# Turning fp16 halves with DMA transposes on the SP queue instead of fp32 rows on TensorE

## The chip, the cores and the metric

The kernel runs on one core of one Trainium2 chip. Its time is the device time of one launch in microseconds (us); the kernel before takes 1377.87 us, the median of 3 runs (1377.47 to 1381.09). Engines are named as in the profile: PE is TensorE's matmul, PEld its weight load, DVE is VectorE, ACT is ScalarE, POOL is GpSimd, SP is SyncE, which here only waits and issues DMAs.

## The reference

16 sequences of 256 tokens with 512 channels, 4096 tokens in all. First a recurrence over the tokens of each sequence (WKV) with the normalised rows as keys and a context as values, added to x. Then, on the normalised result, a shared gated MLP and a routed mixture of 8 experts, of which each token takes 2, with at most 1280 tokens per expert.

```python
x = x + tanh(g_xattn[0]) * wkv(time_decay, time_first, k=layernorm(x), v=ctx_2048)
n = layernorm(x)                                   # (4096, 512)
logits = n @ router                                # (4096, 8)
topk_logits, sel = top_k(logits, 2); cw = softmax(topk_logits)
# row -> (expert, slot), slots in token order, kept while slot < 1280
h = silu(gate) * up;  gate, up = split(buf[e] @ w_up_gate[e])      # 512 -> 2 x 352
routed = sum over the token's 2 experts of cw * (h @ w_down[e])    # 352 -> 512
shared = (silu(gate_s) * up_s) @ shared_w_down                     # 512 -> 2 x 1408 -> 512
x = x + tanh(g_ffn[0]) * (routed + shared)
```

## The kernel before

Tokens are worked in 32 tiles of 128 rows, 8 groups of 4 tiles. Each large product is made from fp16 halves: a value is split into a high fp16 part and the rest (`lo`), and three matmuls (hi·hi, hi·lo, lo·hi) stand for one fp32 product. So the normalised rows are wanted channel-major (channels on the partitions) and split: `xT[:, par, hi/lo, kt, token]`, with two buffers `par` for two groups.

**The attention stage** (up to about 770 us) is a software pipeline that is written out by hand. `group(gs, ga, ...)` on each engine runs the shared MLP of group `gs` and at the same time the recurrence, second norm and routing of group `ga = gs + 1`. It has 15 steps: 11 `up_pair` steps of 24 matmuls of 512 columns and 4 `down_tile` steps of 33. `tiles_at(stage, step)` says which tile does which stage in a step; a tile comes every 3 steps. On PE `attend(done)` puts the small work of the pipeline between the matmuls: at `done == 0` `turn_x` (stage 6), `logits` (stage 7) and `turn_v` (stage 2), at `MID` (18) `turn_y` (stage 4), at `LATE` (21) `turn_k` (stage 0). Each `turn` is 4 fp32 transposes on PE into one of two PSUM banks: `PT` for keys, y and x, `PR` for v and the logits.
After the second norm (`normalise_x2`, DVE, into `xln`) a tile goes: `turn_x` on PE into `PT`, `x_hi` on ACT (`PT` to the high half of `xT`), `x_lo` on DVE (`PT` minus high half), then `logits`, then `choose_experts` on DVE, which reads the logits out of `PR`. The next user of `PR`, `turn_v`, waits for that read (`logits_taken`). SP stores `xln` to DRAM as fp32 rows (`xln_d`) for the experts, and loads x and the context ahead.

**The expert stage** (about 820 to 1320 us) works 8 experts of 1280 slots, each as 5 chunks (`EC`) of 256 slots, 40 chunks in all. POOL gathers 128 rows of a slot tile from DRAM by index (`gather_rows`, line 468), six slot tiles ahead, into two buffers `xg`: even tiles in `wkv`, odd ones in `srng`. A gather waits until the tile two before it in the same buffer has been turned (`xg_turned`). PE runs `up_chunk(j+1)`, `turn_slots(j+2)`, `down_chunk(j)`. `gather_hi` (ACT) and `gather_lo` (DVE) empty the turned rows from `PT`/`PR` into `xgT`. ACT scales each output tile into `ostage` (`stage_out`, line 653), and POOL adds it to `moe_d` in DRAM by an indirect DMA (line 487), in program order with the gathers: gather of tile s+6, wait for staged tile s, add tile s, wait until the add of tile s-1 has landed.
The weights of the next expert come in 11 pieces (`q` = 0 to 10; 8 of `w_up_gate`, 3 of `w_down`) through two staging buffers `wst`: SP loads piece q when piece q-2 has been split (`load_chunk`), ACT makes its high half (`weights_hi`), DVE its low half (`weights_lo`). ACT's and DVE's program in chunk j is: piece 3j, hidden part 0 of chunk j+1, piece 3j+1, hidden part 1, piece 3j+2, hidden part 2, and then `stage_out` of chunk j. SP has nothing else to do in this stage.

At the end the second half of the last group's MLP runs (`half_ups(1)`), and the sum is copied out.

Of the kernel before, what the change touches and what calls it, by code (L numbers as in the profile page):

```python
# [50 lines left out]
MID, LATE = 18, 21  # L51
# [3 lines left out]
def build(nc, x, ctx_in, g_x, g_f, t_decay, t_first, router, w_ug, w_dn, s_ug, s_dn, out):  # L55
    es = ExitStack()
    with es:
# [9 lines left out]
        xln_d = nc.dram_tensor("xln_d", (NTOK, D), F32, kind="Internal").ap()  # L67
# [34 lines left out]
        decay = carve(KT * SEG).rearrange("p (k s) -> p k s", k=KT)  # L102

# [9 lines left out]
        xg1 = carve(D)  # L113
# [3 lines left out]
        xg = [xg1, srng[:, 1, :]]  # L117
        xgT = xT[:, 0, :, :, :].rearrange("p h k (r t) -> p r h k t", r=2)
        sums = wkv[:, 0:HT * D].rearrange("p (j c) -> p j c", j=HT)

# [10 lines left out]
        rt_f = sb("rt_f", [P, KT, E], F32)  # L131
# [24 lines left out]
        sprod = sb("sprod", [P, 2, GT, E], F32)  # L156
        posk = sb("posk", [P, 2, GT], F32)
# [13 lines left out]
        dve_waits = sem("dve_waits"); pool_waits = sem("pool_waits")  # L171
# [12 lines left out]
        x_turned = sem("x_turned"); xhi_ready = sem("xhi_ready"); xlo_ready = sem("xlo_ready")  # L184
# [12 lines left out]
        xg_turned = sem("xg_turned"); xg_hi = sem("xg_hi"); xg_lo = sem("xg_lo")  # L197
# [48 lines left out]
        def _(sp):  # L246
            def load_x(c, k):

                sp.dma_start(acc_tile(c), x_rows[bass.ds(c * P, P), :]).then_inc(x_in[k], 16)
# [4 lines left out]
            def attn_group(g, sums, last=False):  # L254


                for k in range(GT):
# [6 lines left out]
                    sp.wait_ge(xln_ready, c + 1)  # L264
                    sp.dma_start(xln_d[bass.ds(c * P, P), :], xln[k % 2]).then_inc(xln_stored[k % 2], 16)
# [19 lines left out]
            attn_group(0, False)  # L285
# [3 lines left out]
            attn_group(1, False)  # L289
            with sp.Fori(2, GROUPS - 1) as n:  # L290
                attn_group(n, True)
            attn_group(GROUPS - 1, True, last=True)
# [17 lines left out]

            for q in range(WCH):
                load_chunk(0, 0, q)
                if q == 1:
                    start_sums(GROUPS - 2)
            for q in range(WCH):
                load_chunk(1, 1, q)
            with sp.Fori(1, E // 2) as i:
                for p in range(2):
                    for q in range(WCH):
                        load_chunk(2 * i + p, p, q)  # L320
# [24 lines left out]
        def _(pool):  # L345
# [110 lines left out]
            for r in range(2):  # L456
                pool.wait_ge(xln_stored[r], 16 * TILES // 2)
            pool.sem_inc(stage_free, 2)
# [6 lines left out]
            def gather_rows(e, p, s, first):  # L465
                if not first:
                    wait_alone(xg_turned, ET * e + s - 1)
                pool.indirect_dma_start(  # L468
                    out=xg[s % 2], out_offset=None, in_=xln_d,
# [38 lines left out]
        def _(act):  # L508
# [57 lines left out]
            def group(gs, ga, gpar, first=False, last=False):  # L566

                for s in steps_of(first):
                    if ga is not None:
                        for k in tiles_at(6, s):  # L570
                            x_hi(ga, k, first, 1 - gpar)
# [53 lines left out]
            def gather_hi(e, p, j):  # L625

                cc = EC * e + j
                for t in range(2):
                    act.wait_ge(xg_turned, 2 * cc + t + 1)
                    if not (isinstance(e, int) and cc < 2):  # L630
                        act.wait_ge(eup_ready, IT * (cc - 1))
                    T = (PT, PR)[t]
                    act.activation(xgT[:, (p + j) % 2, 0, :, t * P:(t + 1) * P],
                                   T[:, :].rearrange("p (k t) -> p k t", k=KT), ACT.Copy).then_inc(xg_hi, 1)

# [19 lines left out]
            def expert(e, p, half, last=False):  # L655


                for j in range(EC):
# [8 lines left out]
                    if j + 2 < EC:  # L667
                        gather_hi(e, p, j + 2)
                    elif not last:
                        gather_hi(e + 1, 1 - p, j + 2 - EC)  # L670
# [3 lines left out]
            gather_hi(0, 0, 0)  # L674
# [5 lines left out]
            gather_hi(0, 0, 1)  # L680
# [11 lines left out]
        def _(pe):  # L692
# [8 lines left out]
            def turn_k(c, k, first):  # L701
# [3 lines left out]
                elif not (first and k == 0):  # L705
                    pe.wait_ge(xlo_ready, c if k == GT else c - 1)
# [13 lines left out]
            def turn_y(c, k):  # L720
# [3 lines left out]
                else:  # L724
                    pe.wait_ge(xlo_ready, c)
                turn(PT, nd[:, 0].rearrange("p k t -> p (k t)")).then_inc(y_turned, 1)

            def turn_x(c, k):
                pe.wait_ge(xln_ready, c + 1)
                turn(PT, xln[k % 2]).then_inc(x_turned, 1)  # L730

            def logits(g, k, par, route):

                c = GT * g + k
                pe.wait_ge(xlo_ready, c + 1)
# [75 lines left out]
            def group(gs, ga, gpar, first=False, split=False, last=False):  # L811
                if gs is not None:
                    pe.wait_ge(xlo_ready, GT * gs + GT)
                for s in steps_of(first):
# [3 lines left out]
                    if gs is None:  # L818
                        for done in (0, MID, LATE):
# [20 lines left out]
            def turn_slots(e, p, j):  # L840
                cc = EC * e + j
                for t in range(2):
                    s = 2 * j + t
                    pe.wait_ge(gathered[t], 16 * cc + 16)
                    if not isinstance(e, int) or cc > 0:
                        pe.wait_ge(xg_lo, 2 * cc)
# [469 lines left out]
```

## Time and profile before

| | |
|---|---|
| median of the runs | 1377.87 us (1377.47 to 1381.09) |
| span of the profiled execution, first to last instruction | 1378.7 us |
| PE busy | 1276.0 us, 93% |
| DVE busy | 824.8 us, 60% |
| ACT busy | 457.5 us, 33% |
| POOL busy | 477.8 us, 35% |
| TensorE clock granted | 0.996 of full, mean |

The times of the runs surround the span of the profiled execution: its 1378.7 us lie 0.8 us above the median, and nothing that needs adding lies around it. Busy time is a union of intervals for each engine. A timeline row is: start, length, engine, line, operation, tiles out and in, count, and in brackets the idle time before it with the work that ended it. A row of the chain of waits is start, length, what. On DMA rows the last number is the median from issue to landing.

### The profile page before, as it was taken

How to read it: one execution, taken by the hardware profiler on the slowest of the kernel's cores; microseconds unless marked ns; L12 is line 12 of the kernel's file. 1: busy time of each engine (PE TensorE's matmuls, PEld its weight loads, DVE VectorE, ACT ScalarE, POOL GpSimd, SP SyncE). 2: the span in 40 equal slices, each digit the busy share in tenths (PEclk: the TensorE clock that was granted, in tenths of full speed). 3: DMA queues.
4: the chain of work that ended last, by engine and by line, in shares of the span. 5: the costliest groups of instructions: out<-in, count | busy, mean ns of one | idle time of the engine just before them, and what ended most of it. 6: DMA issues, size and time to landing. Idle time of an engine off the chain costs nothing. (4 is left out here: it accounts for less than half of the span.)

```text
span 1378.7 us, 22718 instructions
## 1 busy us (share of the span) xinstructions
PE 1276.0 (93%) x8139; PEld 805.4 (58%) x8139; DVE 824.8 (60%) x1615; ACT 457.5 (33%) x840; POOL 477.8 (35%) x461
## 2 busy tenths in 40 slices
PE   1267999999999999999999899999999999999999
PEld 1233444444444444444444667778778777877766
DVE  6988868768678688688687434343434344343312
ACT  3324214223123133133141224444444444444321
POOL 5533142242232232421421313344434443443320
PEclk9999999999999999999999999999999999999999
DMA  7322012021021111120010324465556555554455
GB/s 203 120 84 77 31 25 68 31 70 46 10 70 46 24 55 45 24 77 32 9 54 26 66 78 107 102 139 112 122 109 132 110 118 120 117 121 93 85 122 183
DMA packets 67195, 112.62 MB, mean 82 GB/s; under 512 B 9166, under 2 KB 30694, under 8 KB 66961
## 3 DMA queue, kind: packets, MB, share of 16 engines
q0 software_dynamic: 20064, 42.19, 16.8%
q1 hardware_dynamic: 37376, 62.67, 15.0%
q10 hardware_dynamic: 9648, 6.31, 1.7%
q8 instruction: 71, 1.16, 0.4%
q14 instruction: 36, 0.29, 0.1%
HBM read 72.19 MB, written 46.81 MB: 86 GB/s over the span
## 5 line engine op out<-in xcount | busy, mean ns | idle before, releaser
L771 PE MATMUL PU<-xT,wreg 128*128 128x512 f16 x1848 | 420.6, 381 | 0.1
L771 PEld LDWEIGHTS PU<-xT,wreg 128*128 128x128 f16 x1848 | 179.4, 98 | 194.5 <-issue 3.2
L786 PE MATMUL PD<-wreg,hreg 128*128 128x512 f16 x924 | 204.8, 379 | 0.0
L487 POOL DMA_INDIRECT moe_d<-hreg,eidx x80 | 126.6, 1582 | 111.9 <-ACT hreg L653 92.5
L866 PE MATMUL PU<-xT,wkv 128*128 128x256 f16 (+1 forms) x1440 | 160.5, 273 | 3.5 <-DVE xT L1215 2.4
L866 PE MATMUL PU<-xT,hreg 128*128 128x256 f16 (+1 forms) x1440 | 160.5, 273 | 0.0
L866 PEld LDWEIGHTS PU<-xT,wkv 128*128 128x128 f16 (+1 forms) x1440 | 146.2, 106 | 19.6 <-issue 3.5
L866 PEld LDWEIGHTS PU<-xT,hreg 128*128 128x128 f16 (+1 forms) x1440 | 146.5, 106 | 15.6
L786 PEld LDWEIGHTS PD<-wreg,hreg 128*128 128x128 f16 x924 | 89.1, 98 | 103.0
L1224 DVE SCALAR_TENSOR_TENSOR srng<-PU,srng 128x256 f32<-128x256 f32 (+1 forms) x120 | 50.8, 423 | 164.1 <-ACT srng L644 164.0
L695 PE MATMUL PT<-ident,wkv 128*128 128x128 f32 x384 | 65.3, 297 | 80.7 <-DVE wkv L1036 33.7
L564 ACT ACTIVATE hreg<-srng 128x512 f16<-128x512 f32 x77 | 48.5, 630 | 210.9 <-DVE srng L1081 210.9
L384 POOL TENSOR_TENSOR rstd<-ve,mhalf 128x1 f32<-128x1 f32 x64 | 38.0, 593 | 230.5 <-DVE ve L990 230.4
L695 PEld LDWEIGHTS PT<-ident,wkv 128*128 128x128 f32 x384 | 48.7, 151 | 107.7 <-DVE wkv L1036 41.4
L468 POOL DMA_INDIRECT wkv<-xln_d,eidx x40 | 39.4, 985 | 203.6 <-PE PR L849 190.9
L1033 DVE RECIPROCAL wkv<-wkv 128x512 f32<-128x512 f32 x32 | 107.2, 3350 | 0.2
L644 ACT ACTIVATE srng<-PU 128x256 f32<-128x256 f32 (+1 forms) x120 | 45.8, 382 | 155.3 <-PE PU L866 155.3
L1026 DVE TENSOR_TENSOR_SCAN wkv<-wkv 128x516 f32<-128x516 f32 x64 | 96.6, 1509 | 1.1
L1227 DVE TENSOR_TENSOR wkv<-srng,wkv 128x256 f16<-128x256 f32 (+1 forms) x120 | 50.9, 424 | 57.9 <-ACT wkv L646 57.9
L880 PE MATMUL PD<-hreg,wkv 128*128 128x512 f16 (+1 forms) x360 | 81.1, 379 | 0.9 <-ACT hreg L653 0.9
L653 ACT ACTIVATE hreg<-PD,wslot 128x512 f32<-128x512 f32 x80 | 55.0, 687 | 79.2 <-PE PD L880 72.2
L880 PE MATMUL PD<-wkv 128*128 128x512 f16 (+1 forms) x360 | 81.1, 379 | 0.0
(141 smaller groups left out, 1547.7 us busy)
## 6 DMA issues: line engine op xcount, KB each, us to landing
wkv<-in_L_ffn_w_up_gate SPq DMA_DIRECT2D x64, 176.0 KB, 3.5
acc<-in_x SPq DMA_DIRECT2D x32, 256.0 KB, 3.9
wkv<-in_ctx SPq DMA_DIRECT2D x32, 256.0 KB, 3.7
xln_d<-wkv SPq DMA_DIRECT2D x32, 256.0 KB, 2.0
moe_d<-acc SPq DMA_DIRECT2D x7, 1024.0 KB, 5.1
wkv<-in_L_ffn_w_down SPq DMA_DIRECT2D x16, 256.0 KB, 4.8
acc<-n_L_ffn_shared_w_up_gate ACTq DMA_DIRECT2D x14, 256.0 KB, 3.3
out<-moe_d SPq DMA_DIRECT2D x1, 3584.0 KB, 26.3
```

The lines of the kernel that those rows point to most:

```text
L487: pool.indirect_dma_start(out=moe_d, out_offset=bass.IndirectOffsetOnAxis(ap=eidx[:, p, 1, s:s + 1], axis=0), in_=ostage[s % 2], in_offset ...
L564: act.activation(hh[:, m, 0, :], srng[:, r, :], ACT.Copy).then_inc(hhi_ready, 1)
L653: act.activation(ostage[t], PD[t][:, :], ACT.Copy, scale=wslot[:, bass.ds(2 * cc + t, 1)]).then_inc(ostaged, 1)
L695: mm = pe.transpose(dst[:, kt * P:(kt + 1) * P], src[:, kt * P:(kt + 1) * P], ident[:, :])
L771: mm = pe.matmul(PU[r][gu][:, :], sU[:, m, gu, a, kt, :], xT[:, gpar, b, kt, :], start=(kt == 0 and a + b == 0), stop=(kt == KT - 1 and a ...
L786: mm = pe.matmul(PD[t % 2][:, :], hh[:, j, a, t * P:(t + 1) * P], sD[:, j, b, :], start=(j == 0 and a + b == 0), stop=(j == JT - 1 and a = ...
L866: mm = pe.matmul(PU[r][gu][0:M, 0:CH], eU[p][:, gu, a, kt, m * P:m * P + M], xgT[:, (p + j) % 2, b, kt, :], start=(kt == 0 and a + b == 0) ...
L880: mm = pe.matmul(PD[t][:, :], eh[0:M, (p + j) % 2, m, a, t * P:(t + 1) * P], eD[p][0:M, m, b, :], start=(m == 0 and a + b == 0), stop=(m = ...
L1026: dve.tensor_tensor_scan(scan_out[:, n].rearrange("p k s -> p (k s)"), decay.rearrange("p k s -> p (k s)"), scan_in[:, n].rearrange("p k s ...
L1033: dve.reciprocal(nd[:, 1], nd[:, 1]).then_inc(rcp_done, 1)
L1224: dve.scalar_tensor_tensor(out=esr[r][0:M, :], in0=PU[r][1][0:M, 0:CH], scalar=HS / WS, in1=esr[r][0:M, :], op0=ALU.mult, op1=ALU.mult).th ...
L1227: dve.tensor_tensor(eh[0:M, (p + j) % 2, m, 1, :], esr[r][0:M, :], eh[0:M, (p + j) % 2, m, 0, :], ALU.subtract).then_inc(ehlo_ready, 1)
```

## The change

The normalised rows are split first and turned afterwards, by DMA.

In the attention stage ACT copies `xln` to fp16 (`x_hi`) and DVE subtracts (`x_lo`), both row-major, into `xhl`, 1024 fp16 values a row. SP then issues a DMA transpose from `xhl` straight into `xT` (8 blocks of 128 by 128 in one instruction) and stores `xhl` to DRAM (`xhl_d`, as many bytes a row as before). `turn_x` is gone from PE. `logits` waits for the transpose to have landed and stands at `EARLY` (9 matmuls into its step) instead of 0; `choose_experts` on DVE stands at the end of its step's attention work instead of at the start; `turn_k` and `turn_y` wait for `x2_done` instead of `xlo_ready` on `PT`.

In the expert stage the gathers bring rows of `xhl_d`, and SP turns each gathered tile with a DMA transpose (`turn_rows`). `turn_slots`, `gather_hi` and `gather_lo` are gone from PE, ACT and DVE. SP's weight loads are now written between its transposes, in its program order.

```diff
-        xln_d = nc.dram_tensor("xln_d", (NTOK, D), F32, kind="Internal").ap()
+        xhl_d = nc.dram_tensor("xhl_d", (NTOK, 2 * D), F16, kind="Internal").ap()
...
-                    sp.wait_ge(xln_ready, c + 1)
-                    sp.dma_start(xln_d[bass.ds(c * P, P), :], xln[k % 2]).then_inc(xln_stored[k % 2], 16)
+                    wait_alone(xlo_ready, c + 1)
+                    if k == 0 and has_past:
+                        wait_alone(up_ready, JT * (g - 1))
+                    sp.dma_start_transpose(
+                        xT[:, par, :, :, k * P:(k + 1) * P].rearrange("p h k t -> p (h k) t"),
+                        xhl[k % 2]).then_inc(x_turned[k % 2], 16)
+                    sp.dma_start(xhl_d[bass.ds(c * P, P), :], xhl[k % 2]).then_inc(xln_stored[k % 2], 16)
...
+            def turn_rows(e, p, j, first=False):
+
+                cc = EC * e + j
+                if not first:
+                    wait_alone(eup_ready, IT * (cc - 1))
+                for t in range(2):
+                    wait_alone(gathered[t], 16 * cc + 16)
+                    sp.dma_start_transpose(
+                        xgT[:, (p + j) % 2, :, :, t * P:(t + 1) * P].rearrange("p h k t -> p (h k) t"),
+                        xg[t]).then_inc(xg_turned[t], 16)
...
+            def expert_pair(e):
+                for p in range(2):
+                    for j in range(EC):
+                        if j + 2 < EC:
+                            turn_rows(e + p, p, j + 2)
+                        else:
+                            turn_rows(e + p + 1, 1 - p, j + 2 - EC)
+                        for q in range(IT * j + 2, min(IT * j + 2 + IT, WCH)):
+                            load_chunk(e + p + 1, 1 - p, q)
+                    for q in range(2):
+                        load_chunk(e + p + 2, p, q)
...
             def gather_rows(e, p, s, first):
                 if not first:
-                    wait_alone(xg_turned, ET * e + s - 1)
+                    wait_alone(xg_turned[s % 2], 16 * (EC * e + s // 2))
...
-            def x_hi(g, k, first, par):
+            def x_hi(g, k, first):
...
-                act.wait_ge(x_turned, c + 1)
-                act.activation(xT[:, par, 0, :, k * P:(k + 1) * P], PT[:, :].rearrange("p (k t) -> p k t", k=KT),
-                               ACT.Copy).then_inc(xhi_ready, 1)
+                act.wait_ge(xln_ready, c + 1)
...
+                act.activation(xhl[k % 2][:, 0:D], xln[k % 2], ACT.Copy).then_inc(xhi_ready, 1)
...
-                    pe.wait_ge(xlo_ready, c if k == GT else c - 1)
+                    pe.wait_ge(x2_done, c if k == GT else c - 1)
...
-                if done == 0:
-                    for k in tiles_at(6, s):
-                        turn_x(GT * ga + k, k)
+                if done == EARLY:
                     for k in tiles_at(7, s):
                         logits(ga, k, par, not first)
+                if done == 0:
                     for k in tiles_at(2, s, last):
                         turn_v(ga, k, first)
...
-            def turn_slots(e, p, j):
...
-                pe.wait_ge(xg_lo, 2 * cc + 2)
+                for t in range(2):
+                    pe.wait_ge(xg_turned[t], 16 * (cc + 1))
...
-                    for k in tiles_at(7, s):
-                        choose_experts(GT * ga + k)
                     for k in tiles_at(6, s):
-                        x_lo(GT * ga + k, k, par)
+                        x_lo(GT * ga + k, k)
...
                         weigh_and_scan(GT * ga + k, k, first)
...
+                    for k in tiles_at(7, s):
+                        choose_experts(GT * ga + k)
```

What DVE does in step 4 of a group in the kernel before; L1063 is the first operation of the choice, which frees `PR`, L1041 the adding of the attention result, L1000 the normalising of keys:

```order
L1081 SCALAR_TENSOR_TENSOR srng<-PU,srng 128x512
L1063 TENSOR_REDUCE lt<-PR 128x8
L1065 MAX top<-lt 128x8
...
L1088 TENSOR_TENSOR hreg<-srng,hreg 128x512
...
L1041 SCALAR_TENSOR_TENSOR acc<-PT,gates,acc 128x512
L986 BN_STATS bn<-acc 128x6
...
L1000 TENSOR_SCALAR wkv<-acc,mv,rstd 128x512
```

The same step of DVE in the changed kernel; L1095, L1102, L1058, L1003, L1017 and L1077 are the former L1081, L1088, L1041, L986, L1000 and L1063:

```order
L1095 SCALAR_TENSOR_TENSOR srng<-PU,srng 128x512
L1102 TENSOR_TENSOR hreg<-srng,hreg 128x512
...
L1058 SCALAR_TENSOR_TENSOR acc<-PT,gates,acc 128x512
L1003 BN_STATS bn<-acc 128x6
...
L1017 TENSOR_SCALAR wkv<-acc,mv,rstd 128x512
L1077 TENSOR_REDUCE lt<-PR 128x8
L1079 MAX top<-lt 128x8
```

The choice, which led the step, now stands behind the adding of the attention result and everything that follows from it.

What SP does in the expert stage of the kernel before, at the head of its loop over pairs of experts (L305 loads a piece of `w_up_gate`):

```order
L305 DMA wkv<-in_L_ffn_w_up_gate 128x352
L305 ISA
L305 DMA wkv<-in_L_ffn_w_up_gate 128x352
L301 REGISTER_ALU
L305 ISA
L305 DMA wkv<-in_L_ffn_w_up_gate 128x352
```

And at the same place in the changed kernel (L334 is the transpose of a gathered tile, L321 the load of a piece):

```order
L334 DMA_TRANSPOSE xT<-wkv 128x8x128
L334 DMA_TRANSPOSE xT<-srng 128x8x128
L317 ISA
L321 ISA
L321 DMA wkv<-in_L_ffn_w_up_gate 128x352
L317 REGISTER_ALU
L321 ISA
L321 DMA wkv<-in_L_ffn_w_up_gate 128x352
```

Pieces 2, 3 and 4 (then 5 to 7, then 8 to 10) now stand behind two transposes, the second of which waits for a gathered odd tile (`srng`).

## Rows read from the trace of the kernel before

**Rows 1.** The page: busy time of each engine, share of the span, instructions.

```profile
PE 1276.0 (93%) x8139; PEld 805.4 (58%) x8139; DVE 824.8 (60%) x1615; ACT 457.5 (33%) x840; POOL 477.8 (35%) x461
```

**Rows 2.** Busy time by stretch: one group of the attention stage, the expert stage.

```profile
168.30:264.90 96.60, 93.96 (x496) 46.77 (x495) 75.17 (x146) 25.84 (x37) 29.95 (x32) 1.00 0.16 45
840.00:1320.00 480.00, 479.75 (x3720) 376.84 (x3719) 186.37 (x378) 211.76 (x454) 198.93 (x164) 1.00 0.55 113
```

**Rows 3.** PE's waits in 160 to 740 us: us in total, times, longest.

```profile
PE PT L695 <- DVE xT L1057: 8.5, 7, 1.4
PE PT L695 <- DVE wkv L1036: 6.3, 10, 1.0
```

**Rows 4.** Timeline of PE, steps 3 to 5 of a group.

```profile
401.70 0.60 PE L695 MATMUL PT<-ident,wkv 128*128 128x128 f32 x4
402.13 4.70 PE L771 MATMUL PU<-xT,wreg 128*128 128x512 f16 x21
...
413.32 0.66 PE L695 MATMUL PT<-ident,wkv 128*128 128x128 f32 x4 [0.32 <-DVE wkv L1036]
...
415.10 0.60 PE L695 MATMUL PR<-ident,wkv 128*128 128x128 f32 x4
```

**Rows 5.** Timeline of DVE in the same steps.

```profile
406.80 0.69 DVE L1057 TENSOR_TENSOR xT<-PT,xT 128x512 f16<-128x512 f32 x1 [1.18 <-ACT xT L553]
...
413.78 0.16 DVE L1063 TENSOR_REDUCE lt<-PR 128x8 f32<-128x16 f32 x1
...
415.56 0.75 DVE L1041 SCALAR_TENSOR_TENSOR acc<-PT,gates,acc 128x512 f32 x1
...
417.69 0.55 DVE L1000 TENSOR_SCALAR wkv<-acc,mv,rstd 128x512 f32 x1
```

**Rows 6.** Chain of waits in one chunk of the expert stage: start, length, what.

```profile
957.47 7.86 PE PU L866 x72
965.33 0.44 PE PT L849 x4
965.77 0.44 PE PR L849 x4
966.21 3.89 PE PD L880 x18
```

**Rows 7.** Timeline of ACT and POOL in a chunk.

```profile
1052.83 0.63 ACT L623 ACTIVATE wkv<-wkv 128x512 f16<-128x512 f32 x1 [0.41 <-DMA wkv<-in_L_ffn_w_down]
...
1053.76 0.38 ACT L644 ACTIVATE srng<-PU 96x256 f32<-96x256 f32 x1 [0.29 <-PE PU L866]
...
1054.62 0.42 ACT L646 ACTIVATE wkv<-srng 96x256 f16<-96x256 f32 x1 [0.49 <-DVE srng L1224]
...
1056.67 0.69 ACT L653 ACTIVATE hreg<-PD,wslot 128x512 f32<-128x512 f32 x1 [0.67 <-PE PD L880]
...
1058.20 1.59 POOL L487 DMA_INDIRECT moe_d<-hreg,eidx  x1 [2.23 <-ACT hreg L653]
...
1060.10 1.30 POOL L468 DMA_INDIRECT srng<-xln_d,eidx  x1 [0.30 <-issue]
```

**Rows 8.** DMA issues of the expert stage: count, KB each, us to landing.

```profile
wkv<-in_L_ffn_w_up_gate SPq DMA_DIRECT2D x51, 176.0 KB, 3.6
wkv<-in_L_ffn_w_down SPq DMA_DIRECT2D x14, 256.0 KB, 5.0
...
wkv<-xln_d,eidx POOLq DMA_INDIRECT x37, 3.4
srng<-xln_d,eidx POOLq DMA_INDIRECT x36, 4.5
```

**Rows 9.** DMA issues of the whole run, 256 KB each.

```profile
acc<-in_x SPq DMA_DIRECT2D x32, 256.0 KB, 3.9
...
xln_d<-wkv SPq DMA_DIRECT2D x32, 256.0 KB, 2.0
```

**Rows 10.** Timeline of PE: the first two chunks of products.

```profile
831.04 8.03 PE L866 MATMUL PU<-xT,wkv 128*128 128x256 f16 x72 [2.38 <-DVE xT L1215]
```

More of the change, by code:

```diff
@@ L183, in build @@
         xln_stored = [sem(f"xln_stored{r}") for r in range(2)]
-        x_turned = sem("x_turned"); xhi_ready = sem("xhi_ready"); xlo_ready = sem("xlo_ready")
+        x_turned = [sem(f"x_turned{r}") for r in range(2)]; xhi_ready = sem("xhi_ready"); xlo_ready = sem("xlo_ready")
         logits_ready = sem("logits_ready"); logits_taken = sem("logits_taken"); top_steps = sem("top_steps")
@@ L196, in build @@
         gathered = [sem(f"gathered{r}") for r in range(2)]
-        xg_turned = sem("xg_turned"); xg_hi = sem("xg_hi"); xg_lo = sem("xg_lo")
+        xg_turned = [sem(f"xg_turned{r}") for r in range(2)]
         ew_in = [sem(f"ew_in{r}") for r in range(2)]
@@ L288, in _ @@
                          zeros[:, :].unsqueeze(1).to_broadcast([P, (HT + 2) * KT, P])).then_inc(moe_started, 16)
[L289 to L292, printed above, removed]
+            attn_group(1, False, 1, has_past=False)
+            with sp.Fori(1, GROUPS // 2 - 1) as n:
+                attn_group(2 * n, True, 0)
+                attn_group(2 * n + 1, True, 1)
+            attn_group(GROUPS - 2, True, 0)
+            attn_group(GROUPS - 1, True, 1, last=True)
             def load_chunk(e, p, q):
@@ L314, in _ @@
                     start_sums(GROUPS - 2)
-            for q in range(WCH):
+            sp.wait_ge(up_ready, JT * GROUPS)
+            for j in range(2):
+                turn_rows(0, 0, j, first=True)
+            for q in range(2):
                 load_chunk(1, 1, q)
[L317 to L320, printed above, removed]
+            with sp.Fori(0, E // 2 - 1) as i:
+                expert_pair(2 * i)
+            expert(E - 2, 0)
+            expert(E - 1, 1, last=True)
             for r in range(2):
@@ L812, in group @@
                 if gs is not None:
-                    pe.wait_ge(xlo_ready, GT * gs + GT)
+                    for r in range(2):
+                        pe.wait_ge(x_turned[r], 16 * (GT // 2 * gs + GT // 2))
                 for s in steps_of(first):
@@ L837, in _ @@
             group(GROUPS - 2, GROUPS - 1, 0, last=True)
-            def turn_slots(e, p, j):
[L841 to L846, printed above, removed]
-                    T = (PT, PR)[t]
-                    for kt in range(KT):
-                        mm = pe.transpose(T[:, kt * P:(kt + 1) * P], xg[s % 2][:, kt * P:(kt + 1) * P], ident[:, :])
-                    mm.then_inc(xg_turned, 1)
             def up_chunk(e, p, j):
@@ L890, in expert @@
                         up_chunk(e + 1, 1 - p, 0)
-                    if j + 2 < EC:
-                        turn_slots(e, p, j + 2)
-                    elif not last:
-                        turn_slots(e + 1, 1 - p, j + 2 - EC)
                     down_chunk(e, p, j)
@@ L1239, in expert @@
                             expert_hidden(e + 1, 1 - p, 0, m)
-                    if j + 2 < EC:
-                        gather_lo(e, p, j + 2)
-                    elif not last:
-                        gather_lo(e + 1, 1 - p, j + 2 - EC)
             def half_hidden(h, m):
```

86 lines of the change are left out of this document (36 added, 50 removed).

## The prediction, made before the changed kernel ran

> **What bounds the kernel now.** I read the page first: PE is busy 93% of the span, no other engine over 60% [rows 1]. Split by stretch, a group of the attention stage has a period of 96.6 us with PE busy 94.0 of it and DVE 75.2; in the expert stage PE is busy 479.75 of 480 us, the others less than half, and the DMA engines 0.55 [rows 2]. The chain of waits says the same of the experts: a chunk is 7.86 us of up products, two times 0.44 us of transposes and 3.89 us of down products, 12.63 us from one chunk to the next (957.47 to 970.10), and nothing else is on it [rows 6]. So each transpose taken off PE is worth its own length, as long as nothing else becomes later than PE. Which waits are near PE, the timelines show.
>
> **What leaves PE.** Four fp32 transposes hold PE for 0.43 us between matmuls (401.70 to 402.13) [rows 4]. For 32 tiles that is 13.8 us, and for the 40 chunks 40 x 0.87 = 34.9 us [rows 6]. With `turn_x` goes a wait: `turn_k` waited in `PT` for `x_lo`, 8.5 us in the six groups of that window, 1.4 a group [rows 3]. If nothing came in exchange, the change would be worth about 60 us. ACT and DVE also lose the emptying of 80 gathered tiles; neither bounds that stage, so this counts as nothing.
>
> **Attention stage: the choice comes late.** In step 4 PE starts `turn_y` at 413.32 and wants `turn_v` of the next step at 415.10 [rows 4]. `turn_v` writes `PR`, so it needs the logits taken out. Before, DVE did that at 413.78, and PE did not wait. Now the reduction stands behind L1041 (415.56) and L1000, which ends its turn by about 418.15 (417.69 and 0.46 net) [rows 5]; with 0.2 for the reduction the release is at 418.35, 3.3 us after PE wants it. DVE saves the wait of 1.18 us for ACT at 406.80 [rows 5], but PE comes 0.43 + 0.81 us or so earlier as well, which leaves the difference. In step 7 no key tile is normalised and DVE has caught up during the first wait; bounded by the chain from `turn_y` (0.5 until DVE sees it, 415.56 to 417.69 = 2.1, 0.2 for the reduction, against 1.78 of PE) it is at least 1 us, likely 2. Step 14 is a down tile of 33 matmuls and has the time. So two waits a group, 3.2 + 2.0 = 5.2 us, against 4 x 0.43 + 1.4 = 3.1 saved: +2.1 us a group, about +15 us in seven groups. The bounds are -1.5 a group (two waits of 0.8) and +3.5 (two of 3.3): -10 to +25.
> Behind the waiting `turn_v` on PE stand the next 24 matmuls and, after them, everything DVE and ACT do with them.
>
> **The transpose's landing.** The trace has none. The nearest rows: the same 256 KB stored from SBUF land in 2.0 us, loaded in 3.9 [rows 9], gathered in 3.4 and 4.5 [rows 8]. I call the landing L and take 3.5, nearest to the load, since 256-byte pieces are more work than 2 KB rows; bounds 2.0 and, open above, 8. `x_lo` ends at 407.49 and would be 1.2 us earlier; the logits are wanted 9 matmuls after 408.95, at 410.9 [rows 4, 5]. That leaves 4.6 us: L = 3.5 costs nothing, each microsecond above 4.6 costs one per tile, 28 times. The SP queue has only its loads of x and context behind it, wanted steps later.
> Here the Trainium skill speaks with two voices. "VectorE: DVE Perf Modes", "The three transpose paths", gives a DMA transpose of 128 by 128 as 1309 ns against 390 for TensorE and advises TensorE where PSUM will do; eight blocks in a row would be an estimated 10.5 us. "Advanced Engine Details and Errata", "X-Bar Transpose (TRN2)", says that they are as fast as ordinary DMAs. By the second the sum stands; by the first it is the second rival below.
>
> **Expert stage: a ring through SP's queue.** PE alone would now need 7.86 + 3.89 = 11.75 us a chunk. But SP loads pieces 3j+2 and on behind the transposes of chunk j+2, and the second of these waits for a gather which POOL issues only after the add of slot tile 2j-2. The piece is needed on ACT before hidden part 2, and that stands before `stage_out` of chunk j, which releases the add of slot tile 2j. This is a ring with one turn per chunk, and its length is read off:
> - `stage_out` starts 1056.67, the add starts 1058.20, the gather of the odd tile 1060.10: 3.4 us [rows 7]
> - the gather into `srng` lands: 4.5 us [rows 8]; SP wakes and issues: 0.15, an estimate
> - the transpose keeps SP and its queue from the load for X. An ordinary issue would be 0.35; at worst the load lands behind the whole transpose, 3.5. I take 1.2
> - the load lands: 3.6 us, for `w_down` 5.0 [rows 8]; ACT starts 0.2 later, an estimate
> - the split 0.5 (0.63 for `w_down`), silu to the fp16 copy 1053.76 to 1055.04, 1.3 [rows 7]
>
> Sum 13.7 + X, for piece 8 15.2 + X: with X = 1.2 14.9, 14.9 and 16.4 us, all over 11.75 and over 12.63. Pieces exist only in chunks 0 to 2 of an expert; chunks 3 and 4 run freely. Three turns put `stage_out` 46.2 - 35.25 = 10.9 us behind PE's own pace. PE feels this through the rows: from `stage_out` to the up products that need the tile there are 13.4 us of PE work (1.94 + 7.86 + 3.89 less 0.3), and the path takes 3.4 + 4.5 + 0.15 + L = 11.6; so 1.8 us are absorbed. An expert then takes 58.75 + 10.9 - 1.8 = 67.9 us against 63.15 before: +4.7. Seven experts load pieces for a next one: +33; the last has none and gains 4 x 0.87: -3.5. Together +30 us. In general an expert takes 60.8 + 3X + L. With X = 0.35 and L = 2.0 it is 63.9, the stage +1; with X = 2.5 and L = 5, 73.3, the stage +67.
> In the transition one wait goes: PE waited 2.38 us for the second chunk's rows [rows 10], with 0.87 of transposes before it: -3.
> The first group, without matmuls, follows DVE; the wait for ACT goes, but the logits stand ahead of `turn_y` on PE and wait for L. I count 0.
>
> **Sum.** 1378.7 (span) + 15 + 30 - 3 = 1420.7; the median lies 0.8 below the span: 1420 us, 3.0% slower.
>
> **The rivals.**
> *Faster (0.13).* The mechanism is PE's relief, and it decides as soon as a turn of the ring is so short that 3X + L falls under 2.3, or the odd gather lands as fast as the even one, 3.4 instead of 4.5 [rows 8] (that takes 1.1 off each turn and adds 1.1 to what is absorbed: 4.4 an expert, 31 us). With X = 0.35, L = 2.0 and that gather the stage is about -30; at half of it, with the choice waits at 0.8 us (-10) and the transition, 1378 - 17 - 10 - 3 = 1348 us. For it: PE is the one engine near its limit. Against: the gather's 4.5 is a median of 36 in this very stage.
> *The transpose is slow (0.12).* L = 8, X = 3: the logits wait 3.4 us in 28 tiles, +95; an expert takes 60.8 + 9 + 8 = 77.8, +103 - 3.5. 1378.7 + 15 + 95 + 99 - 3 = 1585 us. For it: 80 of them run on DMA engines that are already 0.55 busy with the experts [rows 2]; against: a plain transfer of this size never takes 8. Eight blocks one after the other, as the skill's figure has it, would be this case.
> *No change (0.06).* X and L at their lower bounds, the stage +1, choice waits of 1.6 us each: 1378 us, within 0.3%, which is what a measurement of this kernel can tell from no change.
> *The forecast (0.69)*, by itself 1388 to 1460.
>
> Faster by over 0.3%: 0.13. Within 0.3%: 0.04, two thirds of the case of no change. Slower: 0.69 + 0.12 + 0.02 = 0.83. The range that holds 8 in 10 reaches from 1382, which leaves out the faster case, to 1490, which leaves out most of the slow transpose.
>
> **What the profile after would show.** The choice: PE idle before the `PR` transposes of `turn_v`, released by L1077, about 2 to 3 us, twice a group, and a group of 98 to 100 us. The ring: chunks of 11.75 us alternating with chunks of 14 to 17 within each expert, ACT idle before the piece 3j+2 and released by a DMA, SP waiting for the gather into `srng`. The transpose: its landing in the DMA rows, 3 to 4.5 us, and the next SP issue about 1.2 us behind it. I am wrong if chunks are 11.75 us throughout, if `turn_v` never waits, or if PE waits for `x_turned` in every tile.

## The result, and the profile after

The changed kernel takes 1440.7 us (median of 4 runs, 1431.0 to 1448.0), the kernel before on the same chip 1377.7 (4 runs). The ratio is 1.045, with a 95% interval of 1.040 to 1.050: slower by 4.5%. The profiled execution of the changed kernel has a span of 1429.2 us, so its trace holds 50.5 us more than the 1378.7 of before. Its runs spread over 1.2%, where those of before agree within 0.3%.

The page of the changed kernel, busy time of each engine, answers to [rows 1]:

```profile
PE 1252.9 (88%) x7691; PEld 758.7 (53%) x7691; DVE 769.3 (54%) x1535; ACT 412.7 (29%) x760; POOL 476.6 (33%) x461
```

PE lost only 23 us of work, although 48.7 us of transposes are gone: part of the rest runs at a lower clock, see below. The next rows show busy time by stretch, one group of the attention stage and the same 480 us of the expert stage as in [rows 2]. A row is: stretch, its length, the busy us and instructions of PE, PEld, DVE, ACT and POOL, and then the granted clock, the busy share of the DMA engines and GB/s.

```profile
269.22:368.33 99.11, 92.93 (x478) 44.59 (x478) 75.16 (x146) 25.86 (x37) 30.01 (x32) 1.00 0.21 54
840.00:1320.00 480.00, 427.64 (x3118) 319.84 (x3117) 126.92 (x285) 156.51 (x354) 179.17 (x151) 0.96 0.80 144
```

PE, busy for 479.75 of 480 us before, now idles for 52 of them. Two things more stand in the last columns: the granted clock is 0.96, not 1.00, and the DMA engines are busy 0.80, not 0.55. Where the 50.5 us lie, from the first row of each part in PE's timeline:

| part, us | before | after | difference | predicted |
|---|---|---|---|---|
| start-up and the first twelve steps of the first group, to the positions of group 0 | 168.35 | 170.65 | +2.3 | 0 |
| attention: from there six groups and the last three steps | 600.75 | 616.69 | +15.9 | +15 |
| first half of the last MLP, to the first expert | 50.65 | 45.23 | -5.4 | 0 |
| expert stage, to the second half | 510.81 | 550.12 | +39.3 | +27 |
| rest | 48.1 | 46.5 | -1.6 | 0 |

The prediction's +15 was for all seven groups. The first one starts at 83.69 before and 84.67 after, so its first twelve steps stand in the first row of the table and grew by 1.3 us. The last three steps of the last group take 21.67 us in both, so the 15.9 us lie in six groups, 2.7 us in each.

**Attention.** PE's waits in 160 to 740 us, as in [rows 3], and the place in PE's and DVE's timelines that answers to [rows 4, 5]:

```profile
PE PR L733 <- DVE lt L1077: 11.6, 4, 2.9
PE PR L733 <- issue: 11.5, 7, 2.7
PE PR L781 <- DMA xT<-wkv: 5.1, 8, 1.5
```

```profile
319.57 0.66 PE L733 MATMUL PT<-ident,wkv 128*128 128x128 f32 x4
320.06 1.46 PE L805 MATMUL PU<-xT,wreg 128*128 128x512 f16 x6
324.45 0.65 PE L733 MATMUL PR<-ident,wkv 128*128 128x128 f32 x4 [2.93 <-DVE lt L1077]
```

```profile
321.42 0.75 DVE L1058 SCALAR_TENSOR_TENSOR acc<-PT,gates,acc 128x512 f32 x1
...
323.56 0.55 DVE L1017 TENSOR_SCALAR wkv<-acc,mv,rstd 128x512 f32 x1
324.02 0.17 DVE L1077 TENSOR_REDUCE lt<-PR 128x8 f32<-128x16 f32 x1
...
332.32 0.63 ACT L619 ACTIVATE hreg<-srng 128x512 f16<-128x512 f32 x1 [1.40 <-DVE srng L1095]
332.86 0.61 ACT L609 ACTIVATE xhl<-wkv 128x512 f16<-128x512 f32 x1
333.50 0.69 DVE L1071 TENSOR_TENSOR xhl<-wkv,xhl 128x512 f16<-128x512 f32 x1 [1.22 <-ACT xhl L609]
```

`turn_v` (the rows with `PR<-ident`) waits for the reduction, which runs after L1058 and L1017, as the prediction had it. The last three rows, two of ACT and one of DVE, were not foreseen: `x_lo` still waits 1.2 us for ACT's `x_hi` (L609), and that one stands behind the fp16 copy L619, which waited for DVE.

**Experts.** PE's timeline over four chunks (L889 are up products, L903 down products), against 12.63 us a chunk in [rows 6]:

```profile
989.99 8.02 PE L889 MATMUL PU<-xT,wkv 128*128 128x256 f16 x72
997.85 4.05 PE L903 MATMUL PD<-wkv 128*128 128x512 f16 x18
1004.68 9.70 PE L889 MATMUL PU<-xT,wkv 128*128 128x256 f16 x72 [2.78 <-DMA xT<-srng]
1014.22 4.05 PE L903 MATMUL PD<-wkv 128*128 128x512 f16 x18
1019.94 5.41 PE L889 MATMUL PU<-xT,wkv 128*128 128x256 f16 x48 [1.67 <-DMA xT<-srng]
...
1035.69 9.70 PE L889 MATMUL PU<-xT,hreg 128*128 128x256 f16 x72 [2.25 <-DMA xT<-srng]
```

Chunks of 11.75 us (978.23 to 989.99) stand beside chunks of 14.69, 15.26 and 15.75. And two of these sets of 72 products take 9.70 us, not 8.03. The ring, on SP's queue, ACT and POOL, answers to [rows 7]:

```profile
1010.37 0.99 POOL L521 DMA_INDIRECT srng<-xhl_d,eidx  x1 [0.30 <-issue]
...
1015.82 1.24 SPq L334 DMA_TRANSPOSE xT<-srng  x1
1017.31 5.33 SPq L325 DMA_DIRECT2D wkv<-in_L_ffn_w_down  x3
1020.79 0.63 ACT L678 ACTIVATE hreg<-wkv 128x512 f16<-128x512 f32 x1 [7.70 <-DMA wkv<-in_L_ffn_w_down]
...
1022.83 0.67 ACT L697 ACTIVATE hreg<-PD,wslot 128x512 f32<-128x512 f32 x1
...
1024.34 1.59 POOL L540 DMA_INDIRECT moe_d<-hreg,eidx  x1 [8.29 <-ACT hreg L697]
...
1026.24 0.98 POOL L521 DMA_INDIRECT srng<-xhl_d,eidx  x1 [0.30 <-issue]
```

From one gather of an odd tile to the next: 5.45 until the transpose is issued, 1.49 until the load behind it is, 3.48 until ACT starts the piece, 2.04 to `stage_out`, 3.41 to the next gather. Together 15.87 us, and the turn before (994.75 to 1010.37) took 15.62. DMA rows of 840 to 1300 us and, below, of 200 to 740, against [rows 8, 9] (count, KB each where the page has it, median us to landing):

```profile
xT<-srng SPq DMA_TRANSPOSE x33, 4.3
wkv<-xhl_d,eidx POOLq DMA_INDIRECT x33, 4.0
srng<-xhl_d,eidx POOLq DMA_INDIRECT x32, 4.7
```

```profile
xhl_d<-xhl SPq DMA_DIRECT2D x11, 256.0 KB, 2.2
...
xT<-xhl SPq DMA_TRANSPOSE x11, 3.1
```

### The profile page after: what moved, and what is told of

It reads as the page before. It is cut to its first block, busy times and chain, and to the rows that moved or that the text cites. A ratio compares the mean times of both kernels' runs of the same rounds, so it can differ in the third digit from the quotient of the medians.

```text
span 1429.2 us, 21720 instructions
## 1 busy us (share of the span) xinstructions
PE 1252.9 (88%) x7691; PEld 758.7 (53%) x7691; DVE 769.3 (54%) x1535; ACT 412.7 (29%) x760; POOL 476.6 (33%) x461
## 2 busy tenths in 40 slices
DMA packets 185462, 141.93 MB, mean 99 GB/s; under 512 B 127437, under 2 KB 148965, under 8 KB 185232
## 4 chain that ended last, share of the span: by engine, by line
PE 24%; DMA 17%; issue 6%; DVE 4%; ACT 3%; SPq 2%; POOL 1%; ACTq 0%; POOLq 0%; DVEq 0%
DMA srng<-xhl_d,eidx 9%; PE PU L889 8%; PE PD L820 4%; PE PD L903 3%; DMA wkv<-in_L_ffn_w_up_gate 3%; PE PU L805 3%; PE PU L925 3%; DMA xT<-srng 2%; PE PD L937 2%; ACT hreg L697 2%; DMA wkv<-in_L_ffn_w_down 2%; SPq L334 2%; DVE wkv L1050 1%; DVE wkv L1043 1%; DVE srng L1229 1%
## 5 line engine op out<-in xcount | busy, mean ns | idle before, releaser
L889 PE MATMUL PU<-xT,wkv 128*128 128x256 f16 (+1 forms) x1440 | 171.1, 283 | 29.5 <-DMA xT<-srng 20.1
L889 PE MATMUL PU<-xT,hreg 128*128 128x256 f16 (+1 forms) x1440 | 168.0, 279 | 24.9 <-DMA xT<-srng 22.8
L889 PEld LDWEIGHTS PU<-xT,wkv 128*128 128x128 f16 (+1 forms) x1440 | 150.2, 110 | 54.0 <-issue 33.1
L889 PEld LDWEIGHTS PU<-xT,hreg 128*128 128x128 f16 (+1 forms) x1440 | 148.7, 109 | 47.7 <-issue 30.2
L619 ACT ACTIVATE hreg<-srng 128x512 f16<-128x512 f32 x77 | 48.5, 630 | 193.2 <-DVE srng L1095 193.2
L1043 DVE TENSOR_TENSOR_SCAN wkv<-wkv 128x516 f32<-128x516 f32 x64 | 96.5, 1508 | 1.1
L455 POOL TENSOR_TENSOR wkv<-wkv 128x512 f32<-128x512 f32 x32 | 37.7, 1177 | 134.1 <-DVE wkv L1043 134.1
L903 PE MATMUL PD<-hreg,wkv 128*128 128x512 f16 (+1 forms) x360 | 81.1, 379 | 0.9 <-ACT hreg L697 0.9
L903 PE MATMUL PD<-wkv 128*128 128x512 f16 (+1 forms) x360 | 81.1, 379 | 0.0
L617 ACT ACTIVATE srng<-PU 128x512 f32<-128x512 f32 x77 | 46.0, 597 | 121.4 <-PE PU L805 121.2
L462 POOL DMA_INDIRECT slot_d<-stw,sidx x64 | 62.3, 973 | 44.1 <-DVE sidx L1162 27.9
L521 POOL DMA_INDIRECT wkv<-xhl_d,eidx x40 | 39.5, 989 | 101.0 <-issue 50.9
```

What stands on the lines that cost most here:

```text
L462: pool.indirect_dma_start(out=slot_d, out_offset=bass.IndirectOffsetOnAxis(ap=sidx[:, 2 * t + k:2 * t + k + 1], axis=0), in_=stw[:, k, t, ...
L617: act.activation(srng[:, r, :], PU[r][0][:, :], ACT.Silu, scale=1.0 / WS).then_inc(silu_done, 1)
L619: act.activation(hh[:, m, 0, :], srng[:, r, :], ACT.Copy).then_inc(hhi_ready, 1)
L889: mm = pe.matmul(PU[r][gu][0:M, 0:CH], eU[p][:, gu, a, kt, m * P:m * P + M], xgT[:, (p + j) % 2, b, kt, :], start=(kt == 0 and a + b == 0) ...
L903: mm = pe.matmul(PD[t][:, :], eh[0:M, (p + j) % 2, m, a, t * P:(t + 1) * P], eD[p][0:M, m, b, :], start=(m == 0 and a + b == 0), stop=(m = ...
L1043: dve.tensor_tensor_scan(scan_out[:, n].rearrange("p k s -> p (k s)"), decay.rearrange("p k s -> p (k s)"), scan_in[:, n].rearrange("p k s ...
```

## The experiments

Two theories at the start. *Ring and late choice*: the experts lose because the weight loads stand behind the wait for the odd gather, the attention stage because the choice holds the bank `PR`. *Contention and landing*: the transposes slow every DMA beside them, and PE waits for their landing. The kernels of the first four ran together, those of the next four, and the last two; each ratio is to the kernel before on the same chip, with its 95% interval. "Experts" is the time from the first up product to the second half of the MLP, and "attention" the second row of the table above, both in the profiled execution.

**1. The loads between the two transposes**

```diff
-                        if j + 2 < EC:
-                            turn_rows(e + p, p, j + 2)
-                        else:
-                            turn_rows(e + p + 1, 1 - p, j + 2 - EC)
-                        for q in range(IT * j + 2, min(IT * j + 2 + IT, WCH)):
-                            load_chunk(e + p + 1, 1 - p, q)
+                        pieces = list(range(IT * j + 2, min(IT * j + 2 + IT, WCH)))
+                        for ts in ((0,), (1,)):
+                            if j + 2 < EC:
+                                turn_rows(e + p, p, j + 2, ts=ts)
+                            else:
+                                turn_rows(e + p + 1, 1 - p, j + 2 - EC, ts=ts)
+                            for q in (pieces[:2] if ts == (0,) else pieces[2:]):
+                                load_chunk(e + p + 1, 1 - p, q)
```

Here `ts` names the tiles that are turned, (0,) the even one and (1,) the odd one.

> The changed kernel, but SP loads pieces 3j+2 and 3j+3 between the two transposes of a chunk, before the wait for the odd gather, and piece 3j+4 behind the second. Ring theory (the loads that stand behind the wait for the odd gather make a ring of 15 to 16 us a turn, and PE, which idles for it, also loses clock): the ring opens, chunks of all three kinds come near 11.75 us, the expert stage falls from 550 us to 475-490 and the kernel from 1440 to 1360-1380. Contention theory (the transposes cost what they cost on the DMA engines, and every load and gather beside them is late, wherever they stand in SP's program): the stage stays within 15 us of 550, the kernel 1430 to 1448.

Measured: 1387.7 us (1382.6 to 1396.2), ratio 1.005 (1.003 to 1.007); experts 497.1 us. PE in 840 to 1320 us:

```profile
840.00:1320.00 480.00, 463.16 (x3519) 354.58 (x3517) 142.04 (x313) 179.47 (x389) 200.58 (x164) 0.99 0.86 156
```

The ring theory holds, contention falls: the DMA engines are busier than in the changed kernel (0.86 against 0.80), since more is done in the same time, and still 53 us are gone and the clock is back at 0.99. The total missed the expected range by 8 us, and the stage, at 497, that of 475 to 490 by 7: PE still waits 11.1 us for turned odd tiles.

**2. The choice first again**

```diff
+                    for k in tiles_at(7, s):
+                        choose_experts(GT * ga + k)
                     for k in tiles_at(6, s):
                         x_lo(GT * ga + k, k)
...
-                    for k in tiles_at(7, s):
-                        choose_experts(GT * ga + k)
```

> The changed kernel, but the choice of experts on DVE stands at the head of its step again, as in the kernel before. Theory 1 (the late choice holds the bank PR, and turn_v waits for it): a group of the attention stage falls from about 99 us to 96-97, below or at the kernel before, and the kernel loses 10 to 20 us. Theory 2 (the transposes' landing, not the choice, sets the attention stage): the group stays at 98.5 us or more and the kernel within 5 us of the changed one. The expert stage stays at 550 us in both.

Measured: 1426.8 us, ratio 1.032 (1.031 to 1.034), 1.2% under the changed kernel; first positions at 168.1 us, attention 601.6 us, experts 555.2. A group took 96.7 us in the mean of six, against 96.5 before and 99.2 in the changed kernel, and the late choice is the whole loss of this stage. But it only comes back to the kernel before (600.75), not below, although PE has 1.4 us of work less in each group and no wait for `turn_x`. PE's waits in 160 to 740 us say what took their place:

```profile
PE PR L781 <- DMA xT<-xhl: 11.0, 6, 1.9
PE PR L781 <- DMA xT<-wkv: 9.4, 11, 1.5
```

**3. Both edits**

The diffs of 1 and 2 together.

> Both edits in one: pieces loaded between the transposes, the choice first. If both theories hold, the gains add, since they fall in different stages: 1345 to 1368 us, below the kernel before. Contention theory: 1420 to 1440, no better than the choice alone.

Measured: 1366.6 us, ratio 0.990 (0.987 to 0.993); attention 602.2 us, experts 495.4. The gains add, and the kernel is 1.0% faster than the kernel before.

**4. The kernel before with the late choice**

The same move of `choose_experts` as in 2, the other way round, made in the kernel before and nothing else.

> The kernel before, with one move alone: the choice of experts stands at the end of its step's attention work on DVE. Theory 1 (the late choice is what costs the attention stage): turn_v waits for L1063 twice a group, the group goes from 96.6 to 101-102 us and the kernel to 1408-1416. Theory 2 (DVE's slack takes it up; the cost in the changed kernel is the transposes' landing): 1378 to 1385.

Measured: 1406.1 us, ratio 1.018 (1.016 to 1.019), 24 us slower and 2 us under the expected range; attention 617.0 us, as in the changed kernel (616.7), start-up +1.9, experts 512.6. PE's waits for `PR` are the same as well, without any DMA transpose in the kernel:

```profile
PE PR L695 <- DVE lt L1063: 11.6, 4, 2.9
PE PR L695 <- issue: 10.6, 7, 2.7
```

A group took 99.2 us in the mean of six and not 101 to 102. The waits are 3.7 us a group and not 5.2, and the group grew by less than its waits, 2.7; no run shows what takes up the rest.

**5. A spare transpose in the ring**

```diff
+                    if t == 1:
+                        if not (first and j == 0):
+                            wait_alone(spare, 16 * cc)
+                        sp.dma_start_transpose(xhl1[:, :].rearrange("p (b t) -> p b t", b=2 * KT),
+                                               wreg[:, 0:2 * D]).then_inc(spare, 16)
```

> The changed kernel with a spare DMA transpose of the same size (into a buffer that nobody reads) behind each odd transpose of the expert stage, ahead of the loads: 40 more. Ring theory: the loads of pieces 3j+2 and on start one more queue hold later (the 1.24 us that the rows show), three turns an expert, seven experts: +26 us in the expert stage (20 to 32), turns of 16.6 to 17.2 us. Contention theory (a transpose costs by what it takes of the DMA engines): +5 to +15 here, and the same again where the loads stand ahead of it.

Measured: 1463.7 us, ratio 1.060 (1.059 to 1.062): 1.5%, some 21 us, above the changed kernel; experts 584.4, but in a profiled execution that is the slowest of its five runs, where that of the changed kernel is the fastest of four. SP's queue (L336 turns a gathered tile, L342 is the spare one):

```profile
1016.50 1.24 SPq L336 DMA_TRANSPOSE xT<-srng  x1
1017.84 1.43 SPq L342 DMA_TRANSPOSE xhl<-wreg  x1
1019.52 6.98 SPq L323 DMA_DIRECT2D wkv<-in_L_ffn_w_up_gate  x3
```

The load is issued 3.0 us behind the odd transpose, not 1.5. The 21 us lie at the lower end of the ring theory's 20 to 32.

**6. The same spare transposes with the ring cut**

The diff of 5 in the kernel of 1.

> The version with pieces 3j+2 and 3j+3 loaded between the transposes (1387.7 us), with the same 40 spare transposes behind the odd ones. Ring theory: only piece 3j+4 stands behind them, which nobody waits for: 0 to +8 us. Contention theory: the same cost as in the ring, +15 us or more.

Measured: 1386.6 us, ratio 1.004 (1.003 to 1.005); experts 499.8. The row of 840 to 1320 us:

```profile
840.00:1320.00 480.00, 459.13 (x3495) 351.34 (x3493) 141.08 (x311) 177.83 (x388) 195.93 (x164) 1.00 0.97 175
```

The DMA engines are busy 0.97 of the time, and the kernel is no slower than that of 1. So 40 more transposes cost 21 us or more where the loads stand behind them, and nothing that can be told where they don't. That is the cleanest evidence for the ring.

**7. A plain copy in the place of the expert transposes**

```diff
-                    sp.dma_start_transpose(
+                    sp.dma_start(
                         xgT[:, (p + j) % 2, :, :, t * P:(t + 1) * P].rearrange("p h k t -> p (h k) t"),
-                        xg[t]).then_inc(xg_turned[t], 16)
+                        xg[t].rearrange("p (b t) -> p b t", b=2 * KT)).then_inc(xg_turned[t], 16)
```

The kernel leaves out the turning of the experts' rows, so its result is wrong and only its time is of use.

> The changed kernel, but in the expert stage a plain DMA copy of the same 256 KB stands in the place of each transpose, with the same waits and in the same order; the rows of the experts are not turned. Ring theory (the place of the loads behind the wait for the odd gather costs most, the hold and the landing of a transpose the rest): X falls from 1.24 to about 0.4 and the landing from 4.2 to 2-3 us, by 60.8 + 3X + L 4 to 5 us an expert: 1400 to 1415 us, still slower than before. Rival (transposing itself, its hold, its landing and its small packets, is the cost): the kernel comes down to 1365-1385 us.

Measured: 1424.7 us, ratio 1.032 (1.031 to 1.034); experts 537.6. A copy holds SP's queue for half as long:

```profile
L334 SPq DMA_DIRECT2D xT<-srng x37: 594/600/613, 845.6 to 1338.3; - x37
```

(min, median and max in ns; the transposes of the changed kernel have 1232/1236/1295.) The step is smaller than expected, 16 us and not 25 or more. One reason is that the hold fell to 0.60 us and not to 0.4; how much hold and landing are worth each, this run does not separate. But it says what was asked. Of the 39.3 us that the stage lost, 26.8 remain with no transpose in it. The place of the loads costs most; that the DMA transposes is the smaller part. The small packets are not what the copy saves: 126158 of the run's packets are under 512 bytes, against 127437 in the changed kernel.

**8. The logits behind `turn_y`**

In the kernel of 3, `EARLY` is 19 instead of 9.

> The version with both edits (1366.6 us), with the logits on PE one matmul behind turn_y (at 19 of 24 matmuls) instead of at 9. If the waits of 0.8 to 1.9 us of the logits for the landing of the transpose are what eats the relief of PE in the attention stage (4.1 us a group), a group falls from 97 to 93-94.5 us and the kernel by 15 to 25 us, to 1342-1352. Rival (DVE, whose program follows PE's PSUM banks, sets the period, and the wait moves to turn_y or turn_v): 1360 to 1368, the wait for the landing replaced by waits for DVE.

Measured: 1385.6 us, ratio 1.005 (1.003 to 1.006), 19 us slower than 3, outside both ranges. PE's and DVE's waits in 160 to 740 us:

```profile
PE PT L736 <- DVE wkv L1056: 35.4, 19, 3.1
```

```profile
DVE lt L1080 <- PE PR L784: 26.9, 24, 2.6
DVE wkv L1074 <- ACT wkv L612: 13.4, 11, 1.2
```

The wait for the landing is gone, and 35 us for DVE have come. DVE's step begins with the choice, which now waits for the logits, and all that DVE does follows. So in the steps with a tile DVE's program seems to have no slack, although DVE is busy only 76% of a group (75.16 of 99.11 us in the changed kernel). That would also explain why PE's relief was worth nothing in 2, and it led to the next kernel.

**9. The high half earlier on ACT**

```diff
                 act.activation(srng[:, r, :], PU[r][0][:, :], ACT.Silu, scale=1.0 / WS).then_inc(silu_done, 1)
+                between()
                 act.wait_ge(h_ready, n + 1)
                 act.activation(hh[:, m, 0, :], srng[:, r, :], ACT.Copy).then_inc(hhi_ready, 1)
...
-                        for k in tiles_at(6, s):
-                            x_hi(ga, k, first)
...
+                    def turn_hi():
+                        for k in tiles_at(5, s):
+                            x_hi(ga, k, first)
```

This is the kernel of 3 with `x_hi` one step earlier on ACT: `turn_hi` is handed to `shared_hidden` as `between`.

> The version with both edits (1366.6 us), with one move on ACT: x_hi stands between the silu and the fp16 copy of the shared MLP's step before, and no longer behind that copy, which waits for DVE. DVE theory (in the steps with a tile DVE's own program, 17.0 us busy of 19.6 and 1.22 of it waiting for x_hi, sets the pace of the attention stage, so PE's relief was worth nothing there): the wait of 1.22 us in front of x_lo goes, the transpose lands as much earlier, a tile cycle falls from 19.6 to about 18.4 us, a group from 97 to 93-95, the kernel to 1338-1354. PE theory (PE's own work and its waits for the landing are the bound): only the part of the landing waits, at most 3 us a group, less where they are spread: 1350-1362.

Measured: 1353.2 us, ratio 0.981 (0.979 to 0.983), the best version; attention 588.6 us (753.82 less 165.21), groups of 93.1 to 96.2, 94.5 in the mean against 96.7 in 3. The total lies in the ranges of both theories, so it does not decide between them alone. PE's waits for the landing fell too, from 19.8 to 9.9 us in 160 to 740 us, 1.7 a group where a group gained 2.3; 10 has the kernel that tells them apart. The gain is half of the 1.22 us in three tiles of four, for there `x_lo` (L1078) now meets POOL:

```profile
320.29 0.66 DVE L1102 SCALAR_TENSOR_TENSOR srng<-PU,srng 128x512 f32<-128x512 f32 x1
320.44 1.18 POOL L460 TENSOR_TENSOR wkv<-wkv 128x512 f32<-128x512 f32 x1 [1.17 <-DVE wkv L1050]
320.87 1.31 DVE L1078 TENSOR_TENSOR xhl<-wkv,xhl 128x512 f16<-128x512 f32 x1
```

It lasts 1.31 us beside a POOL operation, 0.69 in row 333.50 above.

**10. The same move with the logits behind `turn_y`**

The diff of 9 in the kernel of 8.

> The same move on ACT in the version with the logits behind turn_y (1385.6 us). DVE theory: DVE is relieved of 1.22 us a tile here too, the waits of PE for DVE at turn_y (32.5 us in 570) fall to under half, the kernel to 1345-1360, but not below the kernel with the logits at 9, since the choice, and the adding of the attention result behind it, wait for them. If PE is the bound: 1375-1386.

Measured: 1364.8 us, ratio 0.989 (0.987 to 0.991): 5 us above the range, but 21 us under 8 and 12 above 9. PE's waits for DVE fell from 35.4 to 23.2 us, not to under half. In 160 to 740 us PE waits for no landing in 8 or in 10, so what "attention" gained between them, 13.1 us, comes from DVE's relief. The range for a bound by PE (1375 to 1386) is missed by 10 us. The theory that DVE paces the tile steps holds, for the order of 8; for that of 3 it is the likelier reading.

## Why the prediction was right, and where it was not

The forecast was 1420 us by a late choice and a ring through SP's queue. Both mechanisms are shown by kernels that have one of them alone. The time lies 21 us above the forecast and inside both ranges; 8.5 us of that are in the trace (+50.5 against +42), and the rest is how far the median lies above the profiled execution, see the end of this section. Term by term:

- **The choice, +15.** Measured +15.9 in six groups and +1.3 in the first steps of another, together +17.2, and +16.3 with +1.1 where the choice alone was moved (4). The place, the bank and the two waits a group are as predicted (23.1 us in six groups). But the size is right by luck, since two errors cancel. The predicted waits were 3.2 + 2.0 us; the rows show 2.9 and 2.7 at most, 3.9 a group, and a group grew by 2.7, 2.5 of it by the choice (against 2). And the 3.1 us a group "saved" by the transposes were worth nothing, as 2 shows; 8 to 10 point to why: in the steps with a tile DVE sets the pace.
- **"DVE saves the wait of 1.18 us for ACT" failed.** The row of 406.80 names `x_hi`, and the prediction took it to go with PE's transposes. But the cause is ACT's program order: `x_hi` stands behind the fp16 copy of the hidden part, which waits for DVE's L1095 one instruction earlier. So `x_lo` came no earlier, and the 4.6 us of slack before the logits were about 3.4. With a landing of 3.1 us the tiles that came close waited up to 1.5 to 1.9 us. Experiment 9 removes the true cause.
- **The landing, L = 3.5.** Measured 3.1 in the attention stage and 4.3 beside the gathers. The slow transpose (L = 8) is refuted, and the prediction's estimate of 10.5 us for eight blocks one after the other with it.
- **The ring, +30.** Turns of 15.6 and 15.9 us against 14.9 and 16.4, the sum's terms in the rows: gather to transpose 5.45 (predicted 4.65), X 1.49 (1.2), load to ACT 3.48 (3.8, and 5.2 for `w_down`, whose first load landed faster), the rest 5.4 (5.2). X is the hold of 1.24 us and 0.25 of SP's own. 5 and 6 show X by itself: doubled in the ring it costs 21 us, outside it nothing. In 7 the hold is halved, and with what the landing saves that brings back 16.
- **The size, +27 against +39.3.** The mis-sized terms are X, 1.49 instead of 1.2, and L, 4.3 instead of 3.5. With them the prediction's own 60.8 + 3X + L gives 69.6 us an expert instead of 67.9. In PE's timeline six experts, from the first products of the second (894.90) to those of the last (1314.37), take 69.9 us each, where they took 63.2 before. The turn's other terms were off in both directions, as the bullet before this one shows, and cancel in part.
- **PE's clock, not in the sum.** Up products of a chunk took 9.70 us or so instead of 8.03 in ten chunks of the timeline, about 17 us in all. The granted clock of the down products with the wait behind them, of the two parts of the up products that follow, and of products without a wait:

```profile
997.90:1004.60 6.70, 4.00 (x20) 1.60 (x17) 0.00 (x0) 0.00 (x0) 0.98 (x1) 1.00 0.93 189
1004.68:1008.70 4.02, 4.02 (x25) 3.11 (x26) 1.28 (x3) 1.91 (x5) 0.22 (x1) 0.67 0.30 78
1008.70:1014.20 5.50, 5.50 (x49) 5.07 (x47) 2.62 (x6) 2.79 (x7) 4.36 (x5) 0.93 0.82 124
989.99:997.80 7.81, 7.81 (x73) 7.27 (x72) 3.95 (x9) 4.23 (x11) 4.69 (x4) 1.00 0.67 127
```

  PE had been idle for 2.78 us; behind it the mean of 4 us is 0.67, between the two levels of 1.2 and 2.4 GHz. All ten stand behind waits of 2.2 to 4.0 us, but the products behind four other waits, of 2.04, 2.13, 2.34 and 2.60 us, were not slower. That the ring caused it is shown by 1, where the same work has a clock of 0.99; that idle time is what lowers it is read from the rows, and no run varied it alone. Nor may the 17 us be added to the ring's cost:

```profile
1145.14 9.70 PE L889 MATMUL PU<-xT,wkv 128*128 128x256 f16 x72 [2.34 <-DMA xT<-srng]
1154.67 4.05 PE L903 MATMUL PD<-wkv 128*128 128x512 f16 x18
1162.71 9.70 PE L889 MATMUL PU<-xT,wkv 128*128 128x256 f16 x72 [3.98 <-DMA xT<-srng]
```

  Behind eight of the ten the next chunk waits again, here 3.98 us, for a tile that the ring turns; quicker products would have waited that much longer. Only behind two (964.71 and 1035.69) does it not, which by this reading leaves about 3 us of the 39.
- **The transition, -3.** The wait of [rows 10] is gone: the first two chunks' products take 19.6 us (832.57 to 852.19) against 23.9 before.
- **Start-up, 0.** The first group's products start 1.0 us later, and its first twelve steps take 1.3 longer; in the kernel with the choice alone (4) it is 0.9 and 1.1.
- **The first half of the MLP, 0.** It is 5.4 us shorter. There PE waited 3.57 us for a load of the slot table before, at a clock of 0.93, and 0.68 after, at 1.00, and 0.87 us of transposes are gone. The gain is luck: in 1 to 3 this part takes 51.0 to 51.4 us, as before.

One sum of the rivals has a slip: half of the faster case's 30 us is 15, not 17, which makes its time 1350 us instead of 1348.

Not explained: the median lies 11.5 us above the profiled execution's span, which belongs to the fastest of the four runs, where the prediction put it 0.8 below. The changed kernel and its variants spread by 0.3 to 1.2%, the kernel before by 0.3%, and no run shows which wait varies.

## What to carry to other kernels

Whoever adds an instruction that waits to a DMA queue's program should list what stands behind it, for each of those is now released by that wait too; here the kernel with the same transposes in the same number is 4.5% slower in one order of SP's program and 0.5% in the other. Work taken off the busiest engine is worth something only in the steps where it is also late: find the engine whose program has no slack in each step, and read an idle time of it as its releaser's program order, not as the releaser's input. When a wait is put in front of TensorE, look at what its clock loses behind the wait, and count it only where the next wait does not take it up.

## What the runs showed of the hardware

- A DMA transpose of 128 by 1024 fp16 from SBUF to SBUF holds SP's queue for 1.24 us, a copy of the same bytes into the same pieces 0.60, and lands after 3.1 us in quiet stretches, 4.3 beside gathers. A store of as many bytes lands after 2.2.
- The 80 transposes of the expert stage raise its DMA share from 0.55 to 0.80, and all 112 the packets under 512 bytes of the whole run from 9166 to 127437. Beside them the gathers of odd tiles went from 4.5 to 4.7 us, those of even tiles from 3.4 to 4.0. Plain copies with as many small packets (126158) gave 0.70.
- DVE's subtraction of two SBUF tiles took 1.31 us beside a POOL operation (9), 0.69 alone. The Trainium skill, "GPSIMD Engine Reference", "Specifications", says that POOL's access to SBUF is shared with VectorE and that DVE instructions with two SBUF inputs contend; the trace agrees.
- TensorE's clock: 9.70 us for 72 products behind ten waits of 2.2 to 4.0 us, 8.03 without a wait; behind four other waits, of 2.0 to 2.6 us, they were not slower.
